# Expert blocks begun inside the last slots of a graph layer, closer pairs, and fixed places for the edge groups (one Trainium2 core)

## The reference

```python
norm = w * rsqrt(deg_out[src] * deg_in[dst] + 1e-12)
def gcn(x, W, b):                       # one graph layer
    return relu(segment_sum((x @ W)[src] * norm[:, None], dst) + b)
x = x + gcn(gcn(layernorm(x), W6, b6), W7, b7) @ Wp + bp
# mixture of 8 experts, 2 per row, on the layer-normed rows
xn = layernorm(layernorm(x)) * gamma + beta
w  = softmax(top2(xn @ Wr + br))        # spread over the 8 experts
x  = x + sum_e w[:, e] * (gelu(xn @ W1[e] + b1[e]) @ W2[e] + b2[e])
```

## Time and profile before

| | us |
|---|---|
| median of 3 executions | 3775.18 (3773.27 to 3778.09) |
| the profiled execution: device time | 3771.15 |
| its span | 3769.3 |

### The profile page before, as it was taken

The page is one execution under the profiler, slowest core; times in us unless marked ns, Lnnn a source line. Parts: engine busy times, 40 slices in busy tenths (PEclk is TensorE's granted clock), DMA queues, the critical chain, the costliest instruction groups (busy, mean ns, idle before and its releaser), DMA issues.

```text
span 3769.3 us, 58587 instructions
## 1 busy us (share of the span) xinstructions
PE 2954.2 (78%) x17257; PEld 2010.3 (53%) x17257; DVE 1995.1 (53%) x7494; ACT 1383.3 (37%) x3705; POOL 1993.6 (53%) x2006
## 2 busy tenths in 40 slices
PE   4577289988999999996588888888988664588885
PEld 3456145555555555553355565555655422477775
DVE  7999886777676777751202333333433354333332
ACT  5577355555555555542301111111111110344443
POOL 0000177655555566666277777777777773233332
PEclk9979699999999999998889999888988765799998
DMA  3001355555445555557456666666666642233334
GB/s 102 0 18 36 90 168 164 163 162 164 152 135 162 161 164 165 162 175 232 121 166 211 202 202 200 202 200 201 197 200 201 214 124 72 56 58 58 58 58 106
DMA packets 208606, 535.63 MB, mean 142 GB/s; under 512 B 42924, under 2 KB 138436, under 8 KB 202052
## 3 DMA queue, kind: packets, MB, share of 16 engines
q0 software_dynamic: 105936, 263.26, 28.1%
q1 hardware_dynamic: 99796, 253.82, 19.3%
q10 hardware_dynamic: 2592, 15.16, 1.0%
HBM read 380.42 MB, written 158.05 MB: 143 GB/s over the span
## 4 chain that ended last, share of the span: by engine, by line
PE 38%; DVE 20%; DMA 16%; issue 10%; ACT 7%; POOL 6%; DVEq 2%; SPq 1%; ACTq 0%; POOLq 0%
PE bank L1722 15%; DMA acc<-arena 8%; PE bank L1714 6%; POOL arena L805 6%; DMA zrow<-zsum 5%; ACT arena L1452 3%; DVE arena L942 3%; PE bank L1748 3%; PE bank L1746 3%; PE bank L1736 2%; ACT arena L1460 2%; DMA zsum<-zc 2%; PE bank L1768 2%; PE bank L1863 2%; DVE arena L1112 1%
## 5 line engine op out<-in xcount | busy, mean ns | idle before, releaser
L805 POOL DMA_INDIRECT arena<-table,src_i x1792 | 1723.6, 962 | 843.2 <-issue 514.3
L1722 PE MATMUL bank<-arena 128*128 128x257 f32 x4704 | 1215.6, 394 | 5.5 <-ACT zcd L1469 5.5
L1722 PEld LDWEIGHTS bank<-arena 128*128 128x128 f32 x4704 | 876.7, 196 | 227.6 <-issue 103.4
L1460 ACT ACTIVATE arena<-arena 128x128 bf16<-128x128 bf16 x1440 | 482.4, 393 | 295.9 <-DVE arena L1094 293.6
L1714 PE MATMUL bank<-arena 128*128 128x343 bf16 x2160 | 441.7, 314 | 187.3 <-ACT arena L1460 144.6
L1112 DVE TENSOR_TENSOR arena<-arena,bank 128x343 f32 x720 | 365.7, 508 | 346.9 <-PE bank L1714 266.0
L1714 PEld LDWEIGHTS bank<-arena 128*128 128x128 bf16 x2160 | 180.7, 97 | 428.4 <-issue 199.8
L852 POOL DMA_INDIRECT acc<-arena x105 | 167.8, 1598 | 347.0 <-ACT arena L1567 240.2
L1736 PE MATMUL bank<-arena,s_all 128*32 128x257 f32 x3584 | 265.3, 417 | 70.3 <-DMA arena<-table,src_i 55.5
L1686 PE MATMUL bank<-arena 128*128 128x150 bf16 x1616 | 188.6, 276 | 112.5 <-DVE arena L942 108.9
L1863 PE MATMUL bank<-arena 128*128 128x128 f32 x1680 | 221.3, 286 | 63.8 <-DVE arena L1277 63.6
(11 more groups left out here) (216 smaller groups left out, 3416.1 us busy)
## 6 DMA issues: line engine op xcount, KB each, us to landing
chunks<-arena SPq DMA_DIRECT2D x24, 3307.5 KB
arena<-chunks SPq DMA_DIRECT2D x22, 3307.5 KB, 13.3
arena<-table,src_i POOLq DMA_INDIRECT x1792
zsum<-zc SPq DMA_DIRECT2D x224, 64.2 KB
arena<-sorted_x SPq DMA_DIRECT2D x105, 132.5 KB, 2.1
zrow<-zsum SPq DMA_DIRECT2D x50, 257.0 KB, 4.4
arena<-in_W ACTq DMA_DIRECT2D x16, 512.0 KB, 13.5
arena<-chunks ACTq DMA_DIRECT2D x2, 3307.5 KB, 19.4
```

Of the source, the lines that this page charges most:

```text
L805: pool.indirect_dma_start(gat[:, r, j, :], None, table[L], bass.IndirectOffsetOnAxis(ap=src_i[:, col:col + 1], axis=0)).then_inc(gathered[ ...
L1460: last = act.activation(parts[:, r, i], ohl[:, r], ACT.Copy, scale=w3f[:, i, t:t + 1])
L1722: last = pe.matmul(ps_ap, adj[:, c % 2, h, 0:P], xp[:, h], start=(h == 0), stop=(h == XB_ALL - 1))
```

## The change

Three things are changed together.

1. **Layer 1's groups** stand at fixed tiles of a chunk, four in each: sums at tiles 0, 1, 13, 16, combinations at 1, 2, 15, 18, matrices (now for the group two ahead) at 6, 9, 20, 24. TensorE does a tile's combination before its sums; ACT does a tile's zeroing before its copies, and copies the sums in the tile in which they are made.
2. **Pairs** start every three slots at the closest, so stage 3 of one may share a slot with stage 0 of the next; the slots run to 117. The last pairs start at slots 105, 111 and 114. A pair's sends are issued by twos, five and six slots after its start, without waiting for each other, except those of the last pair and the first of each.
3. **Experts' blocks** 0 to 11 run in slots 112 to 117, two in each, beside the last two pairs. After pair 22 (the 23rd) DVE lists 85 whole blocks, which hold no rows of the last two pairs and no fill; after the last pair it lists the other 20. The fills are written between the loads of blocks 40 to 48. For this PSUM is divided anew: one bank for the blocks' transposes and one for their outputs instead of two each, and the second bias shares the projection's bank, with the waits that go with it.

```diff
-GROUP_AT = [7 * s + 2 for s in range(GPI)]
-COMBINE_AFTER = 3
+SUMS_AT, COMBINE_AT, MATRIX_AT = (0, 1, 13, 16), (1, 2, 15, 18), (6, 9, 20, 24)
...
-PAIR_SLOTS = 4
+PAIR_SLOTS, PAIR_EVERY = 4, 3
...
-BLOCKS = 105
-SEND_LAG = 7
+BLOCKS, LATE_PAIRS, PER_SLOT, FILL_FROM = 105, 2, 2, 40
+SEND_LAG = 5
...
-        ps_b2 = split(bank[5][:, :], PT)
+        ps_b2 = split(bank[3][:, :], PT)
...
-        ps_xe = [split(bank[6 + i][:, 0:KD * P], KD) for i in range(2)]
-        ps_h = [split(bank[2 + i][:, :], HC) for i in range(2)]
-        ps_y = [bank[4 + i][:, 0:D] for i in range(2)]
+        ps_xe = split(bank[0][:, 0:KD * P], KD)
+        ps_h = [split(bank[i][:, :], HC) for i in (2, 5)]
+        ps_y = bank[1][:, 0:D]
...
+        def groups_at(places, t):
+            c, u = divmod(t, CT)
+            return [4 * c + places.index(u)] if u in places else []
...
-                slot += PAIR_SLOTS
+                slot += PAIR_EVERY
...
+        WHOLE = ceil_div((NPAIR - LATE_PAIRS) * PT * P * 2 - NE * (P - 1), P)
+        FRONT = PER_SLOT * (SLOTS - L1_GROUPS)
+        LISTED_AT = STARTS[NPAIR - LATE_PAIRS - 1][0] + PAIR_SLOTS - 1
...
# SP, experts
+            for j in range(FRONT + XB_RING, BLOCKS):
+                if j == FILL_FROM:
+                    sp.wait_ge(sent, 16 * 2 * PT * NPAIR)
+                    sp.wait_ge(pay0_made, 1)
+                    sp.wait_ge(counted, 2)
+                    sp.dma_start(sorted_x[FILL:FILL + P, :], pay0[:, :]).then_inc(filled, 16)
+                if FILL_FROM <= j < FILL_FROM + NE:
...
+                if j == WHOLE:
+                    sp.wait_ge(filled, 16 * (1 + NE))
+                load_block(j)
...
# POOL, layer 2
-                for n in range(SLOTS + SEND_LAG):
-                    if n < L1_GROUPS:
-                        gathers(1, n)
-                    turn = STAGE_AT.get(n - SEND_LAG)
-                    if turn:
-                        i, _, q = turn
-                        send(i, i % 2, q)
+                for n in range(L1_GROUPS):
+                    gathers(1, n)
+                    for i, half in SENDS_AT[n]:
+                        for q in range(half * PT, half * PT + PT):
+                            send(i, i % 2, q)
+                for n in range(L1_GROUPS, SLOTS):
+                    for j in blocks_at(n):
+                        add_block(j)
+                    for i, _, s in STAGES_AT[n]:
+                        if s == PAIR_SLOTS - 1:
+                            for q in range(2 * PT):
+                                send(i, i % 2, q)
...
# DVE, layer 2: the blocks' weights before the pairs' stages
+                if n == L1_GROUPS:
+                    weights_ready()
+                if n >= L1_GROUPS:
+                    experts(blocks_at(n))
+                for i, b, s in stages:
                     pair_stage(i, b, s, i % 2, i // 2, i - 1 if i > 1 else None)
+                if n == LISTED_AT:
+                    list_whole()
...
# ACT, layer 1
-                        if u - 1 in GROUP_AT:
-                            copy_sums(0, it * GPI + GROUP_AT.index(u - 1))
-                        if u - COMBINE_AFTER in GROUP_AT:
-                            n = it * GPI + GROUP_AT.index(u - COMBINE_AFTER)
-                            copy_rows(0, n)
                         if c >= 0:
                             chunk_copies(c, step)
+                        for n in groups_at(COMBINE_AT, it * 2 * CT + u):
+                            copy_rows(0, n)
+                        for n in groups_at(SUMS_AT, it * 2 * CT + u):
+                            copy_sums(0, n)
...
# PE
-                    pe.wait_ge(x1_ready, b)
+                    pe.wait_ge(acc_ready, b)
...
-                pe.wait_ge(acc_ready, i)
+                pe.wait_ge(x1_ready, i + 1)
...
+            def tail_slot(n, stages):
+                first, second = blocks_at(n)
+                if n == L1_GROUPS:
...
+                    block_T(0)
+                block_step(first)
+                for i, _, s in stages[:-1]:
+                    stage_first(i, i % 2, s)
+                    stage_last(i, s)
+                for i, _, s in stages[-1:]:
+                    stage_first(i, i % 2, s)
+                block_step(second)
+                for i, _, s in stages[-1:]:
+                    stage_last(i, s)
...
             def block_T(j):
                 pe.wait_ge(xe_in[j % XB_RING], 16 * (j // XB_RING) + 16)
-                if j > 1:
-                    pe.wait_ge(xe_ready, j - 1)
+                if j:
+                    pe.wait_ge(xe_ready, j)
...
             def block_down(j):
...
-                if j > 1:
-                    pe.wait_ge(y_ready, j - 1)
+                if j:
+                    pe.wait_ge(y_ready, j)
...
+            def block_step(j):
+                if j + 1 < BLOCKS:
+                    block_T(j + 1)
+                block_up(j)
+                if j:
+                    block_down(j - 1)
```

More of the change, by code:

```diff
@@ L316, in gnn_moe_kernel @@
         jump = moe(NE)
-        passed, jumps = (w1_e[:, i].rearrange("p k h -> p (k h)").rearrange("p (e j) -> p e j", e=NE)
-                         for i in range(2))
+        taken = moe(NE)
+        list_from = moe(NE + 1)
         first_f = moe(P)
@@ L724, in layer2_slot @@
                         store_rows(1, CHUNKS - 1)
-                    if stage and stage[2] == PAIR_SLOTS - 1:
-                        store_acc(stage[0], stage[1])
+                    if n == L1_GROUPS:
+                        first_blocks()
+                    for j in blocks_at(n):
+                        load_block(j + XB_RING)
+                    for i, b, s in stages:
+                        if s == PAIR_SLOTS - 1:
+                            store_acc(i, b)
                 layer2_slots(layer2_slot)
@@ L1239, in pair_stage, with layer2_slot @@
                     first_output(i)
-            def layer2_slot(n, c, j, g, stage):
+            def layer2_slot(n, c, j, g, stages):
                 if n + 1 < L1_GROUPS:
@@ new lines, in block_table @@
+                link(dve.scalar_tensor_tensor(out=first_f[:, 0:n], in0=at, scalar=float(P), in1=first_f[:, 0:n],
+                                              op0=ALU.mult, op1=ALU.add))
+                link(dve.tensor_scalar(first_f[:, 0:n], first_f[:, 0:n], list_from[:, 0:1], None, ALU.add))
+                dve.tensor_scalar(exp_i[:, first:first + n], exp_f[:, 0:n], float(NE - 1), None, ALU.min)
+                dve.tensor_scalar(first_i[:, first:first + n], first_f[:, 0:n], float(FILL), None, ALU.min
+                                  ).then_inc(counted, 1)
@@ new lines, in block_table @@
+                if whole:
+                    link(dve.scalar_tensor_tensor(out=taken, in0=ends, scalar=-1.0, in1=n_blk, op0=ALU.mult, op1=ALU.add))
+                    link(dve.tensor_scalar(taken, taken, float(n), 0.0, ALU.add, ALU.max))
+                    link(dve.tensor_tensor(taken, taken, n_blk, ALU.min))
+                    link(dve.scalar_tensor_tensor(out=list_from[:, 0:NE], in0=taken, scalar=float(P),
+                                                  in1=list_from[:, 0:NE], op0=ALU.mult, op1=ALU.add))
+                    assert link.n == WHOLE_STEPS, link.n
@@ L1292, in block_weights, with experts_of, weights_ready @@
                 dve.tensor_copy(row_e[:, j % XB_RING], xe[:, j % XB_RING, PAY - 1:PAY]).then_inc(cols_made, 1)
-            def experts():
+            def experts_of(blocks):
+                _, of = nc.values_load_multi_w_load_instructions(
+                    exp_i[0:1, blocks[0]:blocks[-1] + 1], [mybir.EngineType.DVE], min_val=0, max_val=NE - 1,
+                    skip_runtime_bounds_check_because="exp_i is clamped to 0..7 where it is made")
+                return of
+            def weights_ready():
                 dve.wait_ge(counted, 1)
@@ L1297, in experts @@
                 dve.wait_ge(w2_in, 16 * NE)
-                for j in range(BLOCKS):
-                    if j % LOADED == 0:
-                        _, of = nc.values_load_multi_w_load_instructions(
-                            exp_i[0:1, j:min(j + LOADED, BLOCKS)], [mybir.EngineType.DVE], min_val=0, max_val=NE - 1,
-                            skip_runtime_bounds_check_because="exp_i is clamped to 0..7 where it is made")
-                    block_weights(j, of[j % LOADED])
+            def experts(blocks):
+                for j in blocks:
+                    if (j - blocks[0]) % LOADED == 0:
+                        of = experts_of(blocks[j - blocks[0]:][:LOADED])
+                    block_weights(j, of[(j - blocks[0]) % LOADED])
             def slow_layer(L):
@@ L1411, in _ @@
                     pair_stage(NPAIR - 1, NPAIR - 1, s, 0, NPAIR - 1, NPAIR - 1)
-            block_table()
-            experts()
+                list_whole()
+                weights_ready()
+                experts(range(FRONT))
+            list_rest()
+            dve.wait_ge(counted, 2)
```

(5 more changed lines are left out.)

204 lines of the change are left out of this document (123 added, 81 removed).

## The result

The change made the kernel slower by 0.7%: 3789.8 us median of 14 runs (3778.6 to 3802.1) against 3765.6 (3755.6 to 3778.1, 14 runs) for the kernel before, ratio 1.0068, 95% interval 1.0051 to 1.0084. The forecast was 3700, with 3668 to 3750 as its range; the time lies outside, on the side that had 0.05. The profiled execution of the kernel after has a span of 3776.7 us, 7.4 more than before's 3769.3, and is the shortest of its 14; so the two traces show some 17 us less of the loss than the medians (24.3), and are read for where time goes, not for the sum.

What follows compares the result with a forecast made beforehand. Bounds: TensorE in layer 1 (90% busy), GpSimd in layer 2, chained scatters in the experts' stage. Layer 1 -49, tail +33 - 61 = -28; sum -77, taken as -75 from 3775: 3700 us, range 3668 to 3750.

Steps and rivals of the forecast that it cites:

- Layer 1, the step that failed: Layer 1's loop: groups at new places cut a chunk from 51.04 to 49.0 us, 49 us over 24 chunks.
- The 0.4: Layer 1, tile 4 to next tile 29: 0.4 us added for matrices at new tiles and the later chunk store.
- own sign of being wrong: Wrong if layer 2's gathers are longer, the blocks' period grows, or layer 1's chunk time stays above 50.5 us.
- slower rival: Layer 1's turn: a group's store lands late in each chunk; at 8.7 us landing +142, 3840 us; chance 0.05.
- The turn: Layer 1, around a chunk's change: 10.6 us from the build of tile 29 to that of tile 4.
- the late copy: Layer 1's turn: ACT's copy of the second group's rows waits for the first group's store to land, ending at 9.9 us.
- The lower bound for layer 1: Layer 1: if copy and zeroing cost 1.5 us more each, the 49 us gain falls to about 0.
- Layer 2's gathers: Layer 2 up to slot 96: no change, since GpSimd bounds it and gathers and sends are as many.
- Slots 96 to 111: End of layer 2: pair 19 starts at 2996.2 instead of 3008.66, pairs take 32.5 us, last gather ends at 3136.
- Six slots with twelve blocks: Blocks beside the last two pairs: 49 + 9 + 25 + 13 + 3 = 99 us, last pair finished 33 us later.
- The changes of table: Six slots: ACT switches between gelu and tanh four times more, 1.28 us each, 5 us, 3 counted on the path.
- The end: Last pair's output to last addition: block 11's scatter at +17.9, block 12 at +33, then 92 periods; 61 us less.

Runs made afterwards that it cites:

- old groups, loads of 15: The kernel after with layer 1's groups as before and 15 offsets in a load, at tiles 0 and 15: 3742.7 us, 0.9930 of before.

## Why the prediction was wrong

*Layer 1, the step that failed.* "Afterwards two groups are left there: 33.3 + 4.7 = 38.0. I add 0.4." The stretch from tile 4 to the next tile 29 took 52.8 - 9.4 = 43.4 us instead of 38.4. The 0.4 was to pay for the matrices' new places and the store's, and nothing was put down for the register load. Measured, moving the first two matrices gives back 1.7 us a chunk, and moving the loads instead 3.5 (ten offsets each) or 4.5 (fifteen); the two gains overlap at the step to tile 10, which took 6.6 us in the mean, 5.2 with the matrix moved and 1.9 with the load elsewhere. The prediction saw that the chunk's store leaves later, but asked only whether the zeroing at tile 12 must wait for it. It did not ask what else stands on the path while 3.3 MB move. The cost is shown by removal: with loads of 15 clear of the packets a chunk is 48.4 us, and layer 2 starts at 1827.7 instead of 1876 to 1878, which is about the forecast's 49 us. The prediction's own sign of being wrong, a chunk above 50.5, came true; its slower rival (a late landing at the turn) did not happen.

*The base of that step was wrong too.* The prediction took 8.7 + 40.4 = 49.1 us from one chunk and compared its 49.0 with the mean of 51.04. Chunks of the kernel before come in two kinds. The one after the earlier trace rows, from its build at tile 29 to that at tile 4 and on to the next tile 29:

```profile
1067.05 0.60 PE L1714 MATMUL bank<-arena 128*128 128x343 bf16 x3
...
1075.66 0.61 PE L1714 MATMUL bank<-arena 128*128 128x343 bf16 x3
...
1120.46 0.60 PE L1714 MATMUL bank<-arena 128*128 128x343 bf16 x3 [0.56 <-ACT arena L1460]
```

It takes 53.4 us, 44.8 of them behind tile 4, with three sums and four combinations. In its own kind the forecast saved 0.1 us. Worked through for both kinds in the prediction's way, a chunk comes to about 50.6 and the gain to some 11 us (an estimate: the stretch without groups is 33.3 and 36.5, in the mean 34.9; to it come 4.7, 0.4 and 10.6). That 38.5 us are measured there once the loads are clear, for 38.4 forecast, is luck: the working had no loads in it, though the kernel before spent 4.0 us on a step that takes 2.0 without one (old groups, loads of 15). That the layer as a whole then starts 49 us earlier is luck too: the 22 chunks give 2.7 us each, some 59, and the first two chunks, which the forecast counted like the others, lose 11.

*The turn*: 9.4 us for 10.6. TensorE waits for ACT only 10.0 us in the whole loop (69.1 before), so the late copy costs less than feared. The lower bound for layer 1 does not come out of its terms, though: 1.5 us more in each chunk is 36 us and leaves 13 of the 49, and twice that is 72 and leaves less than nothing; "about 0" is neither.

*Layer 2's gathers*: from the first to the last 1258.7 us (before 1253.8), 5 more where nothing until slot 96 and 6 behind it were forecast.

*Slots 96 to 111*: pairs 19 to 22 begin 38.3, 31.7 and 31.8 us apart; forecast 32.5 each. The first is no shorter than before. But pair 19 itself begins 1105.0 us after layer 2's start (3033.24 - 1928.24), where 1120 were forecast (2996 - 1876), and so the late first step costs nothing. TensorE then waits 6.2 and 10.9 us for the rows of the last two groups, and pair 23 starts 1266.5 us after layer 2 (3194.74 - 1928.24) where the forecast had 1270 (3146 - 1876). The two rows of waits and pair 23's first product:

```profile
3177.36 1.94 PE L1841 MATMUL bank<-arena,s_all 128*32 128x257 f32 x16 [6.19 <-DMA arena<-table,src_i]
...
3192.87 1.94 PE L1841 MATMUL bank<-arena,s_all 128*32 128x257 f32 x16 [10.91 <-DMA arena<-table,src_i]
3194.74 1.12 PE L1861 MATMUL bank<-ident,zr_all 128*128 128x128 f32 x4
```

*Six slots with twelve blocks*: from the end of pair 23's projection (3199) to the last output (3291) 92 us pass instead of 99, at 0.83 of the clock. Four waits of "up" for DVE (4.97, 3.98, 9.65, 5.00) are 24 us, where 25 were counted. The changes of table did not happen, for which 3 us were counted. In the six slots ACT loads a table once, and a tanh follows between gelus without another load:

```profile
3203.74 1.28 ACT L1660 ACT_TABLE_LOAD   x1
...
3226.88 0.20 ACT L1608 ACTIVATE arena<-arena 128x2 f32<-128x2 f32 x1 [1.07 <-DVE arena L1234]
```

The whole trace has four table loads, as the one before. So the 5.5 us that the prediction works out beside its sum for four changes do not arise in this kernel either.

*The end*: block 11's addition comes 16.8 us behind the end of the last output (17.9 forecast), block 12's 30.0 (33), then 92 periods of (3750.69 - 3321.21) / 92 = 4.668 us. The forecast's 4.636 is a miscount: from 3256.18 to 3738.32 there are 103 periods, not 104, that is 4.681 us, and the last 92 of before take 4.669. So one bank instead of two cost nothing that these two traces show.

So two parts of three came out near the forecast (24 us measured for 28, though single terms were off by up to 15), and the third has a gain of 44 us with the loads out of the way, which the load under the store, with the matrix made right ahead of it, turned into a loss of 50. Not settled: by what way the store's packets hold up the load, why a load from a multiple of four is the short one, how the 18 us that the first two chunks are longer divide between the clock and the waits, and what the two chips do on which everything behind a large store is slow.

## What to carry to other kernels

Before work is moved in time, list the places on the path at which an engine reads registers from memory, and how long each such load takes with and without a large transfer beside it; these loads are not in the busy times, and their waits are booked as "issue" or under the name of another engine. Put them where the engine waits anyway, and away from bulk transfers: here that alone was worth 114 us (3789.8 to 3676.0) in a change that looked like a failure. When a forecast starts from one pass of a loop, compare that pass with the mean first: here the pass taken was 2 us short of it, which was the whole gain. A change whose gain is missing may still be right: take out the new collision before it is dropped.

## What was not expected of the hardware

A load of ten offsets into DVE's registers takes 1.07 us if it starts at a multiple of four of the tiles and 2.30 if not, and 3.7 to 4.5 or 5.3 to 6.9 us when it begins 3.7 to 6.8 us behind the issue of a 3.3 MB store; at 8.8 us behind it took 3.6 to 4.2 instead of 2.3, at 11.0 us or more it is not stretched (on chips where the kernel before takes 3766 us). It grows with the values (15: 1.55 or 3.4; four from tile 0: 0.39). A tanh behind a gelu needed no table load. On two other chips the kernel before took 14 and 16% more and the variants of after up to 29% more than 3766 us, with waits of up to 8.5 us of three engines behind the same stores; most of their loads were not stretched, as they began later behind the store.
